# Four fused graph layers on one core: the rounds beside each loop move into it

## The chip, the core and the metric

The kernel runs on one core of a Trainium2 chip. The metric is the device time in microseconds (us) of one execution of the whole program: 2837.21 us, the median of 3 runs (2833.33 to 2839.98). Durations below come from one more execution, the profiled one, which took 2840.6 us, of which 2838.8 us are the span from the first to the last instruction of the program.

The engines are named as in the profile: PE is the matrix engine (PEld its weight loads), DVE, ACT and POOL are the vector, scalar and general engines, SP is the engine that issues the DMAs here.

## What is computed

The input is x of 128 graphs with 64 nodes and 384 features, and a 0/1 adjacency of 64x64 for each graph. Four layers follow one another, each of this form:

```
h = maximum(layernorm(x), 0)
x = x + layer(h, adj)
```

- Layer 0, twice over: `u = h @ (h @ W_left.T).T` above and on the diagonal, the same with `W_right` below it, scaled; `exp(u) * adj` divided by its row sum; times `h @ W_lin.T + b`; layer norm, gain, bias, relu.
- Layers 1 and 2: attention with 12 heads, `q, k, v = h @ Wq.T, h @ Wk.T, h @ Wv.T + bv`, scores `q k / sqrt(384) + bias` with the adjacency as the bias, softmax, times v, then `@ Wo.T + bo`.
- Layer 3, twice over: softmax of `h h / sqrt(384)`, times adj and normalized; three projections of h, one for the part above the diagonal, one for it, one for below; their sum, layer norm, relu.

All is float32. The projections keep float32 accuracy by splitting each operand into a high and a low part and adding three products (`exact_product`, line 229 holds its matmul).

## The kernel before

**Tiles and rounds.** 256 tokens (4 graphs) are a group; there are 32 groups. Two streams (0 and 1) work side by side, each with its own buffers (`wide0`, `ps0` and so on); a round takes one group of each stream, so each layer (a "phase") has ITER = 16 rounds, numbered 0 to 15.

**The order of the work** is written out by hand. For every phase and each of PE, ACT, DVE, POOL there is one line of words (GCN0_ORDERS, ATT_ORDERS, GCN3_ORDERS), each word a stage of one stream; a prime means that the stage belongs to the round before (it is late by one). A BETWEEN line per engine weaves the last late stages of one phase with round 0 of the next. Engines meet only through semaphores, and `Count` works out from the orders which value a wait needs. In the two attention phases the PE's line runs, for each stream, `k2 pv scores` in a row: `pv` (line 1167) and `scores` (line 1136) are 96 small matmuls each in the trace, with 96 weight loads each.

**What is written out and what is looped.** `run_first` emits the not-late stages of round 0. `run_middle` emits round 1, then for phases 0 to 2 `meanwhile` (the split of the next phase's first two weight matrices into high and low part, lines 268 and 276, where PRESPLIT names any: in phases 1 and 2), then round 2, then a hardware loop over rounds 3 to 14, then round 15. Within a loop the round number is in a register, so that each wait against a round's count needs register instructions ahead of it; in a written-out round it is a constant. SP has its own program, `move_program`: it writes out `turn(2)` and loops over 3 to 15. The end of a phase is in `run_between`.

**What each engine runs** is thus, for a phase: round 1, round 2, one loop body passed 12 times, round 15, the between line. PE's copy of a round is by far the longest: 540 matmuls in phase 0, 600 in phases 1 and 2, 404 in phase 3, each with a weight load of its own as an instruction. PE's whole program before the change has 21,828 instructions; ACT, DVE, POOL and SP together have 3,929.

Of the kernel before, what the change touches and what calls it, by code (L numbers as in the profile page):

```python
# [14 lines left out]
ITER = GROUPS // STREAMS  # L15
# [162 lines left out]
def run_middle(eng, order, todo, meanwhile=None):  # L178

    order = [(todo[stage], s, late) for stage, s, late in order]  # L180

    def round_of(r):
        for stage, s, late in order:
            stage(s, r - late)
    round_of(1)
    if meanwhile is not None:
        meanwhile()
    round_of(2)
    with eng.Fori(3, ITER - 1) as r:
        round_of(r)  # L190
    round_of(ITER - 1)


def run_between(line, ended, begun):
# [92 lines left out]
def raw_weights(sp, g, phase):  # L287

    sp.wait_ge(g.hi_split[phase - 1], len(SLOTS[phase - 1]))
    sp.wait_ge(g.lo_split[phase - 1], len(SLOTS[phase - 1]))  # L290
    sp.dma_start(g.w_raw[:], g.weights[phase][:, :STAGED]).then_inc(g.weights_in[phase], 16)


def more_raw_weights(sp, g, phase):

    if len(SLOTS[phase]) > STAGED:
        n = len(SLOTS[phase]) - STAGED
        sp.wait_ge(g.hi_split[phase], n)
        sp.wait_ge(g.lo_split[phase], n)
        sp.dma_start(g.w_raw[:, 0:n], g.weights[phase][:, STAGED:]).then_inc(g.more_weights_in[phase], 16)  # L300


def move_program(sp, g, ph, phases):


    phase, sems, nxt = ph.phase, ph.sems, ph.phase + 1
    before = phases[phase - 1] if phase else None

    def load(s, i, of=phase):
        group = i * STREAMS + s  # L310
        x_in, adj, kinds = g.sources[of]
        if of > phase:
            ph.adj_free(sp, s, ITER - 1)
        elif not isinstance(i, int) or i > 0:
            ph.adj_free(sp, s, i - 1)
        sp.dma_start(g.adjin[s][:, 0:len(kinds)], adj[group][:, kinds[0]:kinds[-1] + 1:kinds.step])\
            .then_inc(g.adj_in[of][s], 16)
        if of > phase:
            ph.x_free(sp, s, ITER - 1)
        elif not isinstance(i, int) or i > 0:  # L320
            ph.x_free(sp, s, i - 1)
        sp.dma_start(g.xin[s][:], x_in[group]).then_inc(g.x_in[of][s], 16)

    def store_and_reload(s, i):
        ph.x_new(sp, s, i)
        sp.dma_start(ph.x_out[i * STREAMS + s], ph.bufs[s].xout).then_inc(sems.stored[s], 16)
        if ph.reload and (not isinstance(i, int) or i + 1 < ITER):
            x_again(s, i + 1)

    def x_again(s, i):  # L330
        sp.dma_start(ph.bufs[s].x, g.sources[phase][0][i * STREAMS + s]).then_inc(sems.x_again[s], 16)

    if phase == 0:
        for s in range(STREAMS):
            load(s, 0)
        for dst, src in ph.params:
            sp.dma_start(dst, src).then_inc(sems.params_in, 16)
    if ph.reload:
        for s in range(STREAMS):
            ph.x_space(sp, s)  # L340
            x_again(s, 0)
    if phase == 0:
        more_raw_weights(sp, g, 0)
    for s in range(STREAMS):
        if before is not None:
            sp.wait_ge(before.sems.stored[s], 16 * ITER + 1)
        load(s, 1)
    if nxt < len(SLOTS):
        for dst, src in phases[nxt].params:
            sp.dma_start(dst, src).then_inc(phases[nxt].sems.params_in, 16)  # L350
        raw_weights(sp, g, nxt)

    def turn(i):
        for s in range(STREAMS):
            store_and_reload(s, i - 2)
            load(s, i)
    turn(2)
    with sp.Fori(3, ITER) as i:
        turn(i)
    if phase and nxt < len(SLOTS):  # L360
        more_raw_weights(sp, g, nxt)
    for s in range(STREAMS):
        store_and_reload(s, ITER - 2)
        if nxt < len(SLOTS):
            sp.wait_ge(sems.stored[s], 16 * (ITER - 2) + 1)
            load(s, 0, of=nxt)
    for s in range(STREAMS):
        store_and_reload(s, ITER - 1)
# [1314 lines left out]
def graph_stack(nc, x, adj, w0, w1, w2, w3, rows0, rows1, rows2, rows3, cols0, cols3, ident, tri, eye, parts,  # L1683
                out):

    with ExitStack() as ctx:
# [56 lines left out]
        def run(eng, k, weights=None):  # L1743

            todo = [dict(ph.stages[k](eng), weights=weights and (lambda m, n=n: weights(n, m)))
                    for n, ph in enumerate(phases)]
            run_first(phases[0].orders[k], todo[0])
            for n, ph in enumerate(phases):
                def meanwhile(to=n + 1):
                    if weights:  # L1750
                        for m in PRESPLIT[to]:
                            weights(to, m)
                run_middle(eng, ph.orders[k], todo[n], meanwhile if n + 1 < len(phases) else None)
                if n + 1 < len(phases):
                    run_between(BETWEEN[n][k], todo[n], todo[n + 1])
            run_last(phases[-1].orders[k], todo[-1])

        @block.sync
        def _(sp):
            sp.dma_start(g.w_raw[:], g.weights[0][:, :STAGED]).then_inc(g.weights_in[0], 16)  # L1760
            for dst, src in g.const_loads:
                sp.dma_start(dst, src).then_inc(g.const_in, 16)
            for ph in phases:
                move_program(sp, g, ph, phases)
            for s in range(STREAMS):
                sp.wait_ge(phases[-1].sems.stored[s], 16 * ITER + 1)
# [94 lines left out]
```

## Time and profile before

| | before |
|---|---|
| median of 3 runs | 2837.21 us |
| lowest, highest | 2833.33, 2839.98 us |
| profiled execution, its span | 2840.6 us, 2838.8 us |
| granted clock of PE, mean over the span | 0.992 of full speed |
| PE busy | 2745.5 us (97%), 34,304 matmuls |
| PEld busy | 2543.5 us (90%) |
| DVE, ACT, POOL busy | 2027.2 (71%), 1283.6 (45%), 1427.2 us (50%) |
| instructions fetched by DMA queue 8 | 85 packets, 1.39 MB |
| instructions fetched by DMA queue 14 | 29 packets, 0.24 MB |

How to read it: busy time is the sum over an engine's own instructions; waits, branches and register instructions are not in it. "issue" as the cause of an idle stretch means that no semaphore ended it: the engine stood still while its sequencer had nothing ready for it. PEclk is the share of full clock that the chip granted PE: 1.0 is 2.4 GHz and 0.5 is 1.2 GHz. Queue 8 and queue 14 carry instructions, not data.

Phase 0 runs from 0 to about 800 us, phase 1 (attention) to about 1400, phase 2 (attention) to about 1985, phase 3 to the end. Windows are cut at the start of PE's loop body, or at the same place of a round that is written out.

### The profile page before, as it was taken

The numbers are of one execution on the slowest core, as the hardware profiler recorded it, in microseconds if no ns is written. First come the engines' busy times: TensorE is split into PE (matmuls) and PEld (weight loads), VectorE is DVE, ScalarE is ACT, GpSimd is POOL, SyncE is SP. The second block draws the span as 40 slices with busy tenths as digits, with TensorE's granted clock in tenths as the row PEclk, the third lists the DMA queues.
The fourth block names the chain that finished last, engine by engine and source line by source line (L and its number), as shares of the span: only waits on it lengthen the run. The fifth ranks groups of instructions, "written<-read, shape, count | busy, mean of one in ns | idle before, by whom it ended". The sixth has DMA issues, their size and how long they took to land.

```text
span 2838.8 us, 85292 instructions
## 1 busy us (share of the span) xinstructions
PE 2745.5 (97%) x34304; PEld 2543.5 (90%) x34304; DVE 2027.2 (71%) x3996; ACT 1283.6 (45%) x2069; POOL 1427.2 (50%) x2507
## 2 busy tenths in 40 slices
PE   6999999999998999999989999999999999999997
PEld 6999999999988999999989999999888888888886
DVE  4666666666686777777767777777677767666776
ACT  3333333333344444444444444444544545445453
POOL 1212112121224555555535555555677777777777
PEclk9999999999999999999999999999999999999999
DMA  4111121211112111111131111112112112111121
GB/s 153 42 62 61 43 79 41 81 41 61 62 54 83 43 48 48 48 49 49 48 100 43 48 48 49 51 51 66 41 39 75 37 37 74 37 64 47 37 74 34
DMA packets 116530, 159.51 MB, mean 56 GB/s; under 512 B 8000, under 2 KB 112320, under 8 KB 116416
## 3 DMA queue, kind: packets, MB, share of 16 engines
q1 hardware_dynamic: 116416, 157.88, 16.9%
q8 instruction: 85, 1.39, 0.2%
q14 instruction: 29, 0.24, 0.0%
HBM read 107.52 MB, written 50.33 MB: 56 GB/s over the span
## 4 chain that ended last, share of the span: by engine, by line
PE 56%; POOL 22%; issue 11%; DVE 5%; ACT 2%; DMA 2%; SPq 1%; POOLq 0%; DVEq 0%; ACTq 0%
PE ps L229 40%; POOL wide L1318 5%; POOL wide L909 4%; POOL wide L900 3%; PE ps L1136 3%; PE ps L1167 2%; PE ps L762 2%; PE ps L1153 2%; PE ps L785 2%; PE ps L702 2%; ACT wide L972 1%; POOL wide L1303 1%; POOL wide L1307 1%; PE ps L1648 1%; POOL x_rstd L867 1%
## 5 line engine op out<-in xcount | busy, mean ns | idle before, releaser
L229 PE MATMUL ps<-w_hi,split 128*128 128x384 f32 x4608 | 1271.8, 344 | 7.6 <-ACT wide L938 4.3
L229 PEld LDWEIGHTS ps<-w_hi,split 128*128 128x128 f32 x4608 | 850.7, 190 | 19.3 <-ACT wide L938 4.7
L229 PE MATMUL ps<-split,w_hi 128*128 128x256 f32 x4608 | 863.8, 283 | 1.6 <-DVE split L619 1.6
L229 PE MATMUL ps<-w_lo,split 128*128 128x384 f32 x2304 | 780.6, 339 | 0.0
L229 PEld LDWEIGHTS ps<-split,w_hi 128*128 128x128 f32 x4608 | 723.8, 189 | 23.9 <-issue 12.7
L229 PE MATMUL ps<-split,w_lo 128*128 128x256 f32 x2304 | 575.6, 280 | 0.0
L229 PEld LDWEIGHTS ps<-w_lo,split 128*128 128x128 f32 x2304 | 438.2, 190 | 1.2 <-issue 1.2
L229 PEld LDWEIGHTS ps<-split,w_lo 128*128 128x128 f32 x2304 | 435.4, 189 | 0.0
L909 POOL TENSOR_TENSOR wide<-wide 128x192 f32<-128x192 f32 x256 | 206.6, 836 | 424.1 <-ACT wide L972 424.1
L1318 POOL TENSOR_TENSOR wide<-wide,row 128x192 f32<-128x192 f32 x512 | 308.9, 637 | 32.5 <-ACT wide L1401 32.5
L496 POOL TENSOR_TENSOR rstd<-mv,pos_half 128x2 f32<-128x2 f32 x64 | 44.2, 699 | 450.6 <-DVE mv L670 450.6
L1401 ACT ACTIVATE wide<-ps 128x768 f32<-128x768 f32 x128 | 103.4, 808 | 250.3 <-PE ps L229 250.3
L900 POOL TENSOR_TENSOR wide<-wide,heads 128x512 f32<-128x512 f32 x128 | 163.2, 1294 | 83.9 <-DVE heads L1040 83.8
L972 ACT ACTIVATE wide<-ps 128x768 f32<-128x768 f32 x64 | 52.0, 812 | 257.2 <-PE ps L229 257.2
L958 ACT ACTIVATE wide<-ps 128x512 f32<-128x512 f32 x192 | 110.1, 598 | 106.7 <-PE ps L1153 62.6
L1053 DVE TENSOR_TENSOR split<-ps,split 128x384 fp32r<-128x384 f32 x128 | 65.4, 553 | 127.5 <-ACT split L967 127.5
L892 POOL TENSOR_TENSOR wide<-xin,bo_row 128x192 f32<-128x192 f32 x256 | 147.4, 605 | 6.3 <-DMA x_after<-wide 6.3
L948 ACT ACTIVATE wide<-wide 128x1536 f32<-128x1536 f32 x64 | 95.3, 1490 | 91.5 <-DVE wide L1023 91.5
L1153 PE MATMUL ps<-ident,wide 128*128 128x128 f32 x768 | 119.2, 282 | 15.0 <-DVE wide L1045 7.2
L1012 DVE TENSOR_TENSOR wide<-ps,bias 128x1536 f32<-128x1536 f32 x64 | 112.0, 1750 | 24.9 <-PE ps L1136 24.9
L923 ACT ACTIVATE wide<-xin,x_shift,x_rstd 128x384 f32<-128x384 f32 x128 | 83.7, 701 | 101.3 <-POOL x_shift L870 101.3
L1464 DVE CAST split<-wide 128x768 fp32r<-128x768 f32 x64 | 42.4, 663 | 113.4 <-ACT wide L1365 68.9
(129 smaller groups left out, 4554.7 us busy)
## 6 DMA issues: line engine op xcount, KB each, us to landing
x_after<-wide SPq DMA_DIRECT2D x96, 384.0 KB, 2.5
xin<-x_after SPq DMA_DIRECT2D x96, 384.0 KB, 3.4
xin<-in_x SPq DMA_DIRECT2D x32, 384.0 KB, 4.3
wide<-in_x SPq DMA_DIRECT2D x32, 384.0 KB, 3.7
wide<-x_after SPq DMA_DIRECT2D x32, 384.0 KB, 4.1
out<-wide SPq DMA_DIRECT2D x32, 384.0 KB, 2.8
w_raw<-in_w SPq DMA_DIRECT2D x4, 2304.0 KB, 12.5
adjin<-in_adj SPq DMA_DIRECT2D x32, 256.0 KB, 3.8
```

The source lines that it names most:

```text
L229: last = nc.tensor.matmul(out, t if tokens_stay else w, w if tokens_stay else t, start=(k == 0), stop=(k == len(pairs) - 1))
L892: ins = nc.gpsimd.tensor_tensor(b.xout[:, rows, at], b.xin[:, rows, at], bo_row[:, at], ALU.add)
L900: nc.gpsimd.tensor_tensor(b.e_rows[:, c * n:(c + 1) * n], b.e_rows[:, c * n:(c + 1) * n], b.factor[:, c * n:(c + 1) * n].unsqueeze(2).broa ...
L909: ins = nc.gpsimd.tensor_tensor(b.xout[:, rows, at], b.xout[:, rows, at], b.o_raw[:, rows, at], ALU.add)
L923: ins = nc.scalar.activation(b.h[:, t], b.xin[:, t], ACT.Relu, bias=b.x_shift[:, t:t + 1], scale=b.x_rstd[:, t:t + 1])
L948: nc.scalar.activation(b.e[:], b.e[:], ACT.Exp, scale=SCALE).then_inc(act_done[s], 1)
L958: nc.scalar.activation(b.pT[:, HPC * c:HPC * c + HPC], b.ps[:, c % 2, :], ACT.Copy)\
L1012: nc.vector.tensor_tensor(b.s[:].rearrange("p c r k -> p r c k"), b.ps[:, :, 0:C * P].rearrange("p r (c k) -> p r c k", c=C), b.bias[:].re ...
L1136: mm = nc.tensor.matmul(b.ps[t * NODES:(t + 1) * NODES, r, c * P + gr * NODES:c * P + (gr + 1) * NODES], b.q[r * HD:(r + 1) * HD, c, at:at ...
L1153: mm = nc.tensor.transpose(b.ps[:, c % 2, r * P:(r + 1) * P], b.e[:, c, r], g.ident[:])
L1318: ins = nc.gpsimd.tensor_tensor(b.hw[:, rows, m, at], b.hw[:, rows, m, at], w_row[l][m][:, at], ALU.add)
L1401: nc.scalar.activation(b.hw[:, :, m], b.ps_w[m], ACT.Copy).then_inc(act_done[s], 1)
```

## The change

The written-out copies of round 2 and round 15 are removed, on all engines and in all four phases, and the loop runs over 2 to 15 in their place; on SP `turn(2)` goes into its loop. Round 0, round 1, `meanwhile` and the between lines stay written out. No stage, tile or dependency changes, and no wait gets another value. The program gets shorter: PE's from 21,828 to 13,172 instructions, those of the other four from 3,929 to 2,649.

```
@@ -185,10 +185,8 @@
     round_of(1)
     if meanwhile is not None:
         meanwhile()
-    round_of(2)
-    with eng.Fori(3, ITER - 1) as r:
+    with eng.Fori(2, ITER) as r:
         round_of(r)
-    round_of(ITER - 1)
 
 
 def run_between(line, ended, begun):
@@ -354,8 +352,7 @@
         for s in range(STREAMS):
             store_and_reload(s, i - 2)
             load(s, i)
-    turn(2)
-    with sp.Fori(3, ITER) as i:
+    with sp.Fori(2, ITER) as i:
         turn(i)
     if phase and nxt < len(SLOTS):
         more_raw_weights(sp, g, nxt)
```

Two places show what stands where. Line numbers of the changed kernel are 2 to 3 lower. The first is ACT in phase 1, around the end of round 1; L268 (L266) is the high part of the next phase's weights, L948 (L945) the exponential, L938 (L935) the copy of q, L923 (L920) the norm. Before, written-out round 2 follows the weights:

```order
L972 ACTIVATE wide1<-ps1 128x768
L948 ACTIVATE wide0<-wide0 128x1536
L268 ACTIVATE w_hi<-w_raw 128x1152 x2
L938 ACTIVATE wide1<-ps1 128x768
L923 ACTIVATE wide0<-xin0,x_shift0,x_rstd0 128x384 x2
L958 ACTIVATE wide0<-ps0 128x512
```

Now the loop begins right behind them, and its first pass is round 2:

```order
L969 ACTIVATE wide1<-ps1 128x768
L945 ACTIVATE wide0<-wide0 128x1536
L266 ACTIVATE w_hi<-w_raw 128x1152 x2
L188 UNCONDITIONAL_BRANCH
L188 ISA
L935 ACTIVATE wide1<-ps1 128x768
L914 REGISTER_ALU
L916 ISA
L920 ACTIVATE wide0<-xin0,x_shift0,x_rstd0 128x384 x2
```

The weights keep their place between round 1 and round 2; the rows that are new behind them are the loop's register instructions. The second place is PE in phase 2, behind the loop's end, from the last product of v on (48 in these rows are 96 matmuls in the trace). Before, this is written-out round 15, with its `pt`, `hT`, `k2`, then `pv` and `scores`:

```order
L229 MATMUL ps1<-w_hi,split1_1 128x384 x3
L1153 MATMUL ps0<-ident,wide0 128x128 x4
L1072 MATMUL ps0<-ident,wide0 128x128 x6
L1153 MATMUL ps0<-ident,wide0 128x128 x8
L229 MATMUL ps1<-split1_0,w_hi 128x256
L229 MATMUL ps1<-split1_0,w_lo 128x256
L229 MATMUL ps1<-split1_0,w_hi 128x256
L229 MATMUL ps1<-split1_0,w_lo 128x256
L229 MATMUL ps1<-split1_0,w_hi 128x256
L229 MATMUL ps1<-split1_0,w_lo 128x256
L229 MATMUL ps1<-split1_1,w_hi 128x256 x3
L1167 MATMUL ps0<-wide0 32x64 x48
```

Now it is the between line to phase 3, which stood one round further down before:

```order
L227 MATMUL ps1<-w_hi,split1_1 128x384 x3
L227 MATMUL ps1<-split1_0,w_hi 128x256
L227 MATMUL ps1<-split1_0,w_lo 128x256
L227 MATMUL ps1<-split1_0,w_hi 128x256
L227 MATMUL ps1<-split1_0,w_lo 128x256
L227 MATMUL ps1<-split1_0,w_hi 128x256
L227 MATMUL ps1<-split1_0,w_lo 128x256
L227 MATMUL ps1<-split1_1,w_hi 128x256 x3
L1133 MATMUL ps1<-wide1 64x64 x48
L1150 MATMUL ps0<-ident,wide0 128x128 x12
L1164 MATMUL ps0<-wide0 32x64 x48
```

One written-out stretch with `pv` and `scores` of both streams is gone from behind the loop, and one from ahead of it.

## Rows read from the trace of the kernel before

**Rows 1.** The page: PE's busy time, and the queue with PE's instructions.
```profile
PE 2745.5 (97%) x34304; PEld 2543.5 (90%) x34304; DVE 2027.2 (71%) x3996; ACT 1283.6 (45%) x2069; POOL 1427.2 (50%) x2507
q8 instruction: 85, 1.39, 0.2%
```

**Rows 2.** Phase 1, rounds 1-4, 15: window, length, PE/PEld/DVE/ACT/POOL busy (count), PEclk, DMA, GB/s.
```profile
837.40:878.10 40.70, 34.81 (x614) 33.45 (x606) 28.50 (x35) 15.94 (x23) 15.95 (x26) 0.94 0.38 123
878.10:926.70 48.60, 39.91 (x601) 38.60 (x601) 30.42 (x37) 18.91 (x26) 17.42 (x30) 0.89 0.12 37
926.70:963.60 36.90, 35.28 (x601) 34.22 (x601) 27.11 (x35) 16.82 (x24) 18.60 (x30) 0.98 0.15 47
963.60:998.50 34.90, 34.68 (x603) 33.59 (x602) 27.46 (x35) 16.77 (x24) 19.61 (x30) 1.00 0.14 40
1348.10:1383.20 35.10, 34.77 (x602) 33.66 (x601) 27.62 (x35) 16.79 (x24) 19.53 (x30) 1.00 0.16 53
```

**Rows 3.** Phase 2, rounds 1, 2, 3, 4, 15, the same columns.
```profile
1424.10:1465.20 41.10, 34.98 (x617) 33.17 (x610) 28.12 (x35) 16.03 (x24) 18.48 (x30) 0.94 0.44 141
1465.20:1507.80 42.60, 37.48 (x601) 36.08 (x600) 29.90 (x37) 18.97 (x26) 18.67 (x30) 0.93 0.15 45
1507.80:1546.30 38.50, 36.31 (x602) 35.25 (x602) 27.80 (x35) 16.71 (x24) 18.60 (x30) 0.95 0.16 53
1546.30:1582.20 35.90, 35.81 (x601) 34.89 (x601) 27.11 (x34) 16.72 (x24) 18.55 (x30) 0.96 0.11 37
1931.80:1968.50 36.70, 34.78 (x602) 33.64 (x601) 27.62 (x35) 16.78 (x24) 19.54 (x30) 1.00 0.25 84
```

**Rows 4.** Phase 1, rounds 1 and 2 (837.4 to 926.7): instruction packets of queue 8.
```profile
q8 instruction: 10, 0.16, 0.8%
```

**Rows 5.** Phase 1, rounds 4 to 14 (963.6 to 1348.1): the same.
```profile
q8 instruction: 1, 0.02, 0.0%
```

**Rows 6.** PEld in time, round 14 of phase 1: start, length, line, count.
```profile
1345.34 1.01 PEld L1167 LDWEIGHTS ps<-wide 64*32 64x32 f32 x96
1346.44 1.12 PEld L1136 LDWEIGHTS ps<-wide 32*64 32x64 f32 x96
```

**Rows 7.** The chain of work, 880 to 930 us: start, length, what.
```profile
884.17 1.16 ACT w_hi L268
885.35 2.81 DVE w_lo L276 x2
...
901.08 2.26 issue
...
921.96 2.90 issue
```

**Rows 8.** PEld's waits, phase 1, 837.4 to 1383.2: total, times, longest.
```profile
PEld ps L1136 <- issue: 11.3, 6, 3.0
```

**Rows 9.** PEld's waits, phase 2, 1424.1 to 1968.5.
```profile
PEld ps L1136 <- issue: 9.6, 5, 2.2
PEld ps L1153 <- DVE wide L1045: 6.0, 12, 3.7
```

**Rows 10.** Phase 0, round 2 (written out) and round 4 (in the loop).
```profile
86.70:136.40 49.70, 49.70 (x542) 45.62 (x541) 33.18 (x89) 19.36 (x37) 10.57 (x24) 1.00 0.18 60
186.00:235.70 49.70, 49.70 (x541) 45.63 (x541) 33.29 (x89) 19.35 (x37) 10.59 (x24) 1.00 0.18 58
```

**Rows 11.** Phase 3, rounds 2, 3 and 14.
```profile
2093.90:2145.70 51.80, 51.03 (x405) 45.10 (x404) 36.61 (x92) 25.86 (x44) 39.23 (x71) 1.00 0.16 52
2145.70:2197.30 51.60, 51.11 (x406) 45.16 (x405) 36.54 (x93) 25.85 (x44) 39.47 (x72) 1.00 0.16 52
2712.00:2763.50 51.50, 51.02 (x407) 45.25 (x406) 36.50 (x92) 25.84 (x45) 39.61 (x75) 1.00 0.15 51
```

**Rows 12.** The loop's own instructions on PE: count, shortest/median/longest in ns.
```profile
L189 PEldq ALU_OP  x48: 32/32/32, 185.7 to 2763.2; - x48
L189 PEldq COMPARE_BRANCH  x48: 76/208/247, 185.8 to 2763.3; - x48
```

More of the change, by code:

```diff
@@ L187, in run_middle @@
         meanwhile()
-    round_of(2)
-    with eng.Fori(3, ITER - 1) as r:
+    with eng.Fori(2, ITER) as r:
         round_of(r)
-    round_of(ITER - 1)
 def run_between(line, ended, begun):
@@ L356, in turn @@
             load(s, i)
-    turn(2)
-    with sp.Fori(3, ITER) as i:
+    with sp.Fori(2, ITER) as i:
         turn(i)
```

## The prediction

> **What bounds the kernel now.** I read the page first. PE is busy 97% of the span [rows 1], at full clock nearly everywhere, so nothing on DVE, ACT or POOL matters unless PE waits for it; the question is where PE's missing 3% lies and whether this change reaches it. The page also lists a queue that fetches instructions: 85 packets for 1.39 MB, 16 KB each [rows 1]. PE's program has 21,828 instructions, so one packet holds about 256 of them, and 85 packets are the program once. PE executes over 68,000 matmuls and weight loads, three times the program. So a loop's later passes are not fetched again.
>
> Next the windows by round. In phase 1 the ordinary round takes 34.9 us (round 4) [rows 2], but round 2 takes 48.6 and round 3 takes 36.9, with the same count of 600 matmuls. In phase 2 rounds 2, 3, 4 and 15 take 42.6, 38.5, 35.9 and 36.7 [rows 3]. The same work is slow at the start of each attention phase and becomes even a few rounds on. The DMA view says what differs: 10 instruction packets arrive in rounds 1 and 2 [rows 4], one in the eleven rounds 4 to 14 [rows 5]. Round 3 is the loop's first pass and is fetched like written-out code.
>
> Then the chain of waits. In round 2 it holds two stretches of "issue", 2.26 and 2.90 us [rows 7], where no semaphore is awaited. Both stand inside `scores`. The waits view adds them up: PEld before L1136 stood on "issue" for 11.3 us in 6 stops in phase 1 [rows 8] and 9.6 us in 5 stops in phase 2 [rows 9]. Why there: `pv` and `scores` together issue 192 weight loads and 192 matmuls in 2.2 us [rows 6]. A packet's worth of instructions is eaten in 1.5 us there, where a whole round of some 1,215 instructions takes 34.9. After such a stop PE's clock falls from 2.4 to 1.2 GHz for a stretch; round 2 of phase 1 has a mean of 0.89 [rows 2], which is 0.11 x 48.6 = 5.3 us of full-speed work lost in that round.
>
> One more thing lies in round 2, and is not the fetch: the split of the next phase's weights, 1.16 us on ACT and 2.81 us on DVE [rows 7], sits ahead of round 2's softmax on their queues; PE's transposes (L1153) wait 3.7 us for it in phase 2 [rows 9].
>
> At the fetch the Trainium skill (Runtime: NRT & Kernel Launch, "Instruction fetch mechanics") says that blocks are 16 KiB, 256 instructions, which agrees with 1.39 MB in 85 packets. It also says that crossing a block's border is mostly hidden; by that this change would be worth nothing. The trace decides against it for code as dense as `pv` and `scores`: stops of 2.26 and 2.90 us.
>
> **Part 1: rounds 2 and 15 are no longer fetched as code of their own.** Time over 34.9 us:
> - phase 1: round 2 13.7, round 3 2.0, round 4 0, round 15 0.2, sum 15.9 [rows 2];
> - phase 2: 7.7, 3.6, 1.0, 1.8, sum 14.1 [rows 3].
>
> Together 30.0 us. The weight split stays (it stands between round 1 and the loop on ACT and DVE in the new order too). It costs about 4.8 us a phase: 3.7 to 4.0 us of wait and some 1 us of half clock behind it; the second number is my choice, from the way round 2 falls behind an ordinary round. That leaves 30.0 - 9.6 = 20.4 us for the fetch, in six fetched rounds (2, 3 and 15 of two phases): 3.4 us each, between 0.2 (round 15 of phase 1) and 8.9 (round 2 of phase 1).
>
> Now round 2 is the loop's first pass, fetched once, and rounds 3 to 15 come from what is held. Fetched rounds go from six to two. At the mean, 2 x 3.4 = 6.8 us remain: 13.6 us less. Bounds: with 0.2 each, 20.0 less; with 8.9 each, 2.6 less.
>
> I checked the mean by position, since a stop can only come where PE reaches the border between two packets. I counted PE's instructions from the start of the program to each load that ended such a stop (the ones after 2.26 and 2.90 us, and eight more in the two phases): all leave the same remainder, 232 or 233, on division by 256. Taking the removed copies out (1,088 instructions each in phase 0, 1,215 in phases 1 and 2) moves the borders. By the new count round 1 of phase 1 keeps one stop of its two, its round 2 gets two small ones (0.9 and 1.6 us), phase 2 keeps both in round 1 and has one of 2.0 and one of 0.4 us in round 2. Stops in all, at the length that the trace's stops have: 11.6 us, where the same count gives 19.6 for the kernel before. With fewer stretches of half clock this comes out at 12 to 15 us. I stay with the mean.
>
> **Part 2: the other phases.** In phase 0 a written-out round takes 49.7 us and one in the loop 49.7 [rows 10]: nothing is lost to the fetch, since its densest stages are short; worth 0. In phase 3 rounds 2 and 3 take 51.8 and 51.6, a later one 51.5 [rows 11]: 0.2 us less at most.
>
> **Part 3: what the loop adds.** Eight more rounds (two in each of four phases) carry register instructions on every engine. On PE the branch takes 208 ns and a register instruction 32 ns [rows 12]; by the program's count a round in the loop has 16 to 26 instructions more, so at most 8 x (0.21 + 26 x 0.032) = 8.3 us if all of it were exposed. Cover: PE's sequencer runs ahead of the matmuls, and the two equal rounds of phase 0 [rows 10], with 26 such instructions in one and none in the other, show 0. I take 0. DVE, ACT and POOL are busy 27, 17 and 20 us of 34.9 [rows 2], so their register instructions fall into idle time. SP gains one looped turn per phase; its loads are for a round ahead and nothing waits for them there.
>
> **Sum.** -13.6 - 0.2 + 0 = -13.8, rounded to -14. Against the profiled execution, 2840.6 us: 2826.6. The runs' median is 3.4 us below the profiled one, so 2837.2 - 14 = 2823 us.
>
> **Rivals.**
> - *The remaining fetched rounds are the bad ones.* A phase's first rounds are where the raw weights arrive (123 and 141 GB/s in round 1 [rows 2, 3], 37 to 53 later) and packets may be late behind them; round 2 of phase 1 was the worst of all. If the two first passes cost 8.9 and 6 us, or if PE, no longer held up, waits for DVE and ACT instead, the change brings 20.4 - 14.9 = 5 us: 2832. Against it: round 2's own bytes are few (37 GB/s), DVE and ACT have 7 and 18 us to spare.
> - *They are nearly free*, as round 15 of phase 1 was: -20 us, 2817. It needs luck with the borders in both phases.
> - *The register instructions are exposed* in the attention phases, where the queue ahead of PE is emptied in `scores`: 4 rounds x 1 us and some more where a wait's value comes late, up to 8 us of the 14 given back: 2831. Against it: round 4 is a loop round and takes 34.9 us, written-out round 15 of phase 1 35.1 [rows 2].
> - *Slower: a loop no longer stays held.* What is held must cover the loop body (1,232 instructions in attention, 4.8 packets, so up to 6) and what is read beyond its end. If the shifted borders break this for one loop, each of its 13 later passes is fetched: 13 x 3.4 = 44 us, less the 14: 2867. It decides at the point where one pass has to drop the loop's first packet. Against it: both attention loops touch six packets' worth of code before and after, and phase 0's five now instead of six. The Trainium skill's same section speaks for this rival: it says only two blocks are held and that a taken branch out of them forces a fetch before execution goes on. By it the eight added passes would each stop at least once, by the stops seen 8 x 2.3 = 18 us. But 11 passes of a loop of 4.8 packets brought one packet [rows 5], so the trace does not bear that out.
>
> **Chances.** Forecast 0.70, bad ones 0.12, nearly free 0.10, exposed registers 0.05, loop not held 0.03. About 0.2%, 5.7 us, is what a measurement of this kernel can tell from no change. The forecast's own range is 2818 to 2829; the nearly free case lies at 2817 and the bad ones at 2832, so 2816 to 2831 holds 8 in 10. Faster by over 0.2%: nearly all of the forecast, the free case, a third of the others, 0.83. Within: 0.13. Slower: the last rival and a little, 0.04.
>
> **What the changed profile would show.** Queue 8 has 51 or 52 packets (13,172 / 256) and 0.84 MB. Windows: round 2 of the attention phases is still long (38 to 45 us with the weight split), round 3 and round 15 take 34.9 to 35.1. PEld's "issue" before L1133 (1136 before) falls from 11 stops to 5 to 7 in the phases' loops and round 1. Phase 0 and phase 3 keep their length within 0.5 us. The mean granted clock rises from 0.992 to 0.994 or more. I am wrong if round 3 or 15 is still long, if packets arrive during the loops' later passes, or if the time saved there comes back as PE's waits for DVE or ACT.

## The result, and the profile after

The changed kernel took 2827.53 us, the median of 6 runs (2824.36 to 2828.89), beside 2837.59 us for the kernel before on the same chip (6 runs, 2833.33 to 2841.05). The ratio is 0.9956, with a 95% interval of 0.9944 to 0.9968: 9 to 16 us less. Run again in the second group of experiments, it stood at 0.9963 (0.9950 to 0.9976). The forecast of 14 us less is a ratio of 0.9951, inside the first interval and at the edge of the second. The profiled execution took 2825.8 us, 14.8 us less than the profiled one of before; the medians differ by 10 and 9 us. So the direction and the place were right, and the size was some 2 to 4 us too large. The ratios and intervals below leave out three executions, one each of round 15 alone, round 2 alone and all but PE, which took 9203 to 9204 us at full clock, for a reason that no trace here shows.

The page of the changed kernel, the same lines as [rows 1]:

```profile
span 2824.0 us, 86094 instructions
PE 2738.9 (97%) x34304; PEld 2534.4 (90%) x34304; DVE 2026.3 (72%) x3996; ACT 1282.2 (45%) x2069; POOL 1432.6 (51%) x2507
q8 instruction: 51, 0.84, 0.1%
```

PE's fetch has fallen from 85 packets to 51, the number that the prediction worked out from the length of the program. PE is busy for 6.6 us less, though it does the same work. That is about what fewer stretches at half clock would give: from 830 to 2000 us ten such stretches hold 33.6 us of busy PE before and six hold 20.2 us now, and half of the difference is 6.7 us. The mean granted clock rose from 0.992 to 0.995.

The windows of phase 1, rounds 1, 2, 3, 4 and 15, which answer to [rows 2] (length; PE, PEld, DVE, ACT, POOL busy with counts; PEclk; DMA share; GB/s):

```profile
836.10:874.00 37.90, 34.43 (x619) 33.08 (x612) 28.14 (x35) 15.94 (x23) 16.30 (x26) 0.95 0.42 131
874.00:916.40 42.40, 35.61 (x602) 33.55 (x600) 31.23 (x37) 18.97 (x26) 19.83 (x30) 1.00 0.14 43
916.40:950.90 34.50, 34.40 (x601) 33.48 (x601) 26.16 (x35) 16.82 (x24) 18.62 (x30) 1.00 0.13 41
950.90:985.90 35.00, 34.71 (x603) 33.49 (x602) 27.57 (x35) 16.82 (x24) 19.72 (x30) 1.00 0.15 48
1335.50:1370.40 34.90, 34.61 (x601) 33.38 (x600) 27.47 (x35) 16.81 (x24) 19.80 (x30) 1.00 0.15 52
```

The same of phase 2, which answers to [rows 3]:

```profile
1409.70:1451.40 41.70, 35.81 (x616) 34.07 (x609) 27.93 (x35) 16.01 (x24) 17.47 (x30) 0.92 0.46 145
1451.40:1496.60 45.20, 38.44 (x602) 37.12 (x601) 30.40 (x37) 19.06 (x26) 17.42 (x30) 0.92 0.13 42
1496.60:1532.50 35.90, 35.80 (x602) 34.88 (x602) 27.18 (x34) 16.71 (x24) 18.61 (x30) 0.96 0.12 38
1532.50:1567.50 35.00, 34.70 (x601) 33.37 (x600) 27.45 (x35) 16.82 (x24) 19.77 (x30) 1.00 0.15 48
1918.20:1953.30 35.10, 34.80 (x602) 33.47 (x602) 27.55 (x35) 16.82 (x24) 19.78 (x30) 1.00 0.26 86
```

Read the two phases apart. In phase 1 round 2 fell from 48.6 to 42.4 us and its clock rose from 0.89 to 1.00, and round 3 fell from 36.9 to 34.5. In phase 2 round 2 *rose* from 42.6 to 45.2, while rounds 3, 4 and 15 fell by 2.6, 0.9 and 1.6. From the start of round 1 to the end of round 15, phase 1 gave 11.5 us (545.8 to 534.3) and phase 2 only 0.8 (544.4 to 543.6). The start up to round 2 of phase 0 gave 1.3, the rest of phase 0 gave 1.1 and phase 3 lost 0.3. One stop of the kernel before escapes these windows: PEld stood on issue for 1.24 us just behind the cut at 1383.2 (next load at 1384.78), so phase 1 with it gave 12.7.

The changed kernel has a second profile (its run beside the experiments), and what differs between the two is not the change. From round 1 to round 15 of phase 1, then of phase 2, then rounds 2 to 15 of phase 0 and 1 to 15 of phase 3:

```profile
838.90:1373.90 535.00, 522.09 (x9019) 502.97 (x9012) 416.09 (x513) 253.63 (x361) 290.70 (x446) 0.99 0.17 54
1413.30:1954.20 540.90, 522.72 (x9014) 502.43 (x9006) 415.79 (x512) 253.56 (x362) 292.61 (x450) 0.99 0.18 57
86.90:782.50 695.60, 695.60 (x7562) 638.59 (x7561) 466.59 (x1233) 271.24 (x505) 148.31 (x336) 1.00 0.18 58
2028.70:2801.00 772.30, 765.35 (x6062) 677.49 (x6061) 544.61 (x1377) 385.69 (x660) 590.53 (x1079) 1.00 0.15 50
```

Here phase 2 gave 3.5 us, phase 0 nothing (695.6 against 695.0 before), and round 2 was 42.7 us at clock 0.92 in phase 1 and 44.2 in phase 2, round 3 34.6 and 34.9. The long round 2 of phase 2 stands in both profiles; a difference of 1 to 3 us in one phase of one profile does not tell kernels apart.

The waits of PEld in phase 1 and then in phase 2, in total, times, longest (L1133 is now `scores`, L1150 the transposes, L227 the large matmuls), which answer to [rows 8] and [rows 9]:

```profile
PEld ps L1133 <- issue: 2.2, 2, 1.4
PEld ps L227 <- issue: 1.3, 1, 1.3
...
PEld ps L1150 <- DVE wide L1042: 8.1, 14, 4.3
PEld ps L1133 <- issue: 5.3, 3, 1.9
PEld ps L227 <- issue: 1.2, 1, 1.2
```

The stops on "issue" before `scores` fell from eleven, 20.9 us in all [rows 8, 9], to five of 7.5 us; with the two before L227 there are seven, 10.0 us. Four of the seven are in phase 2, and they are long. The trace also shows the packet at each of the seven: PE goes on 1.2 to 1.5 us after a packet of queue 8 has ended. Around the stop that ended at 1495.44, for example, one packet started at 1492.87 and took 1.07 us, and no other of that queue from 1488 to 1495.4. Counted over PE's instructions in the trace, the ends of successive stops within a phase lie multiples of 256 apart, to within two.

Not all of the stops' time came off. PE's own waits on issue before `scores` and the large matmuls fell by 10.3 us in the two phases (19.5 to 9.2), its idle time there by 7.8 us (38.0 to 30.2): some 2.5 us came back as other waits.

### The profile page after: what moved, and what is told of

Its sections match the earlier page's. It is cut to its first block, busy times and chain, and to the rows that moved or that the text cites. A ratio compares the mean times of both kernels' runs of the same rounds, so it can differ in the third digit from the quotient of the medians.

```text
span 2824.0 us, 86094 instructions
## 1 busy us (share of the span) xinstructions
PE 2738.9 (97%) x34304; PEld 2534.4 (90%) x34304; DVE 2026.3 (72%) x3996; ACT 1282.2 (45%) x2069; POOL 1432.6 (51%) x2507
## 4 chain that ended last, share of the span: by engine, by line
PE 51%; POOL 26%; issue 13%; DVE 5%; ACT 3%; DMA 2%; POOLq 1%; SPq 0%; DVEq 0%; ACTq 0%
PE ps L227 37%; POOL wide L1315 6%; POOL wide L906 5%; POOL wide L897 4%; PE ps L1133 3%; PE ps L1164 2%; PE ps L759 2%; POOL wide L1300 2%; PE ps L782 2%; POOL wide L1304 2%; PE ps L1150 2%; ACT wide L969 2%; PE ps L699 2%; POOL x_rstd L864 1%; POOL rstd L1334 1%
## 5 line engine op out<-in xcount | busy, mean ns | idle before, releaser
L227 PE MATMUL ps<-w_hi,split 128*128 128x384 f32 x4608 | 1268.2, 343 | 8.7 <-ACT wide L935 5.5
L227 PEld LDWEIGHTS ps<-w_hi,split 128*128 128x128 f32 x4608 | 846.3, 190 | 23.8 <-ACT wide L935 6.1
L227 PE MATMUL ps<-split,w_hi 128*128 128x256 f32 x4608 | 863.5, 283 | 1.6 <-DVE split L616 1.6
L227 PE MATMUL ps<-w_lo,split 128*128 128x384 f32 x2304 | 777.3, 337 | 1.2 <-issue 1.2
L227 PEld LDWEIGHTS ps<-split,w_hi 128*128 128x128 f32 x4608 | 723.5, 189 | 23.9 <-issue 12.7
L227 PE MATMUL ps<-split,w_lo 128*128 128x256 f32 x2304 | 575.2, 280 | 0.0
L227 PEld LDWEIGHTS ps<-w_lo,split 128*128 128x128 f32 x2304 | 436.0, 189 | 0.0
L227 PEld LDWEIGHTS ps<-split,w_lo 128*128 128x128 f32 x2304 | 435.2, 189 | 0.0
L493 POOL TENSOR_TENSOR rstd<-mv,pos_half 128x2 f32<-128x2 f32 x64 | 44.2, 699 | 448.2 <-DVE mv L667 448.2
L945 ACT ACTIVATE wide<-wide 128x1536 f32<-128x1536 f32 x64 | 95.3, 1489 | 96.2 <-DVE wide L1020 96.2
L1150 PE MATMUL ps<-ident,wide 128*128 128x128 f32 x768 | 119.6, 281 | 16.6 <-DVE wide L1042 7.7
L920 ACT ACTIVATE wide<-xin,x_shift,x_rstd 128x384 f32<-128x384 f32 x128 | 83.7, 701 | 102.0 <-POOL x_shift L867 102.0
L1150 PEld LDWEIGHTS ps<-ident,wide 128*128 128x128 f32 x768 | 87.1, 141 | 37.4 <-DVE wide L1042 13.8
## 6 DMA issues: line engine op xcount, KB each, us to landing
w_raw<-in_w SPq DMA_DIRECT2D x4, 2304.0 KB, 11.5
```

Source lines behind the costliest of these rows:

```text
L227: last = nc.tensor.matmul(out, t if tokens_stay else w, w if tokens_stay else t, start=(k == 0), stop=(k == len(pairs) - 1))
L920: ins = nc.scalar.activation(b.h[:, t], b.xin[:, t], ACT.Relu, bias=b.x_shift[:, t:t + 1], scale=b.x_rstd[:, t:t + 1])
L945: nc.scalar.activation(b.e[:], b.e[:], ACT.Exp, scale=SCALE).then_inc(act_done[s], 1)
L1150: mm = nc.tensor.transpose(b.ps[:, c % 2, r * P:(r + 1) * P], b.e[:, c, r], g.ident[:])
```

## The experiments

The twelve runs (eleven edits, and the changed kernel again) stood beside the kernel before, in groups of four on one chip each. On the three chips the kernel before took 2837.93, 2839.06 and 2843.16 us (medians), so I compare ratios. "Stops" below is what the profile gives as PEld's waits on issue before `scores` and before the large matmuls, from 830 to 2000 us. "Half clock" counts the stretches at granted clock 0.5 in the same time (one of double length counts as two).

| kernel | ratio to before (95%) | span | stops, us | half clock |
|---|---|---|---|---|
| before | 1 | 2838.8 | 22.6 | 10 |
| changed | 0.9956 (0.9944-0.9968) | 2824.0 | 10.5 | 6 |
| changed, again | 0.9963 (0.9950-0.9976) | 2824.6 | 10.5 | 4 |
| round 15 alone | 0.9990 (0.9976-1.0003) | 2832.0 | 17.2 | 9 |
| round 2 alone | 0.9991 (0.9979-1.0003) | 2830.1 | 16.4 | 8 |
| PE alone | 0.9951 (0.9936-0.9967) | 2822.4 | 11.0 | 6 |
| all but PE | 1.0025 (1.0012-1.0038) | 2847.4 | 23.9 | 11 |
| changed, 195 ahead | 0.9949 (0.9936-0.9962) | 2820.0 | 5.4 | 4 |
| changed, 51 ahead | 0.9986 (0.9974-0.9999) | 2836.7 | 14.1 | 9 |
| more written out | 1.0109 (1.0089-1.0129) | 2864.3 | 40.5 | 12 |
| small weight split | 0.9934 (0.9915-0.9952) | 2827.1 | 13.5 | 7 |
| before, 195 ahead | 1.0009 (0.9997-1.0021) | 2841.1 | 20.0 | 11 |
| PE alone, 195 ahead | 0.9924 (0.9906-0.9941) | 2818.1 | 6.5 | 4 |
| changed but DVE | 0.9949 (0.9931-0.9967) | 2825.6 | 12.6 | 6 |

The theory, F: PE stands still where it reaches a packet of instructions that has not arrived; only code run for the first time is fetched, and only in `pv` and `scores` does PE eat a packet faster than the next arrives. The rivals are named in the expectations.

**Which engine.** The change was made on PE alone (k is 0 for PE, 1 for ACT, 2 for DVE, 3 for POOL), and then on all engines but PE, with `looped=k != 0` and SP's loop as in the changed kernel:

```
+    if looped:
+        with eng.Fori(2, ITER) as r:
+            round_of(r)
+        return
     round_of(2)
     with eng.Fori(3, ITER - 1) as r:
...
-                run_middle(eng, ph.orders[k], todo[n], meanwhile if n + 1 < len(phases) else None)
+                run_middle(eng, ph.orders[k], todo[n], meanwhile if n + 1 < len(phases) else None,
+                           looped=k == 0)
```

> The change on PE alone: its rounds 2 and 15 go into its loop; ACT, DVE, POOL and SP keep theirs written out. Theory F: all of the change is PE's fetch, so the time is that of the changed kernel, 9 to 12 us less than before, with 51 packets on queue 8 and 29 on queue 14. Theory R (the other engines' part): 0 to 3 us less.

> The change on all engines but PE, whose program stays as before. Theory F: within 2 us of before, 85 packets on queue 8. Theory R (the other engines' part): most of the 10 us less. If the register instructions of the loop cost something on ACT, DVE or POOL, this one is slower than before by it.

PE alone has the whole gain: 0.9951, 13.9 us less by the ratio, which is above the 9 to 12 expected, though its interval and the changed kernel's nearly coincide. All engines but PE is slower than the kernel before, 7 us by the ratio, where F had at most 2: a miss. So the gain is PE's, as F says, and with PE's rounds written out the looped form on the others is not free. But the two do not add up: -13.9 and +7 would make 7 us less, and the changed kernel has 10.5 to 12.5 less. What the others cost beside a looped PE is then less than 7 us, and why it is more beside a written-out one stays open. The part that its trace shows plainly is DVE's, and it is taken up below.

**Which round.** From the kernel before, only round 15 moved into the loop, or only round 2 (with SP's turn 2):

```
-    with eng.Fori(3, ITER - 1) as r:          -    round_of(2)
-        round_of(r)                           -    with eng.Fori(3, ITER - 1) as r:
-    round_of(ITER - 1)                        -        round_of(r)
+    with eng.Fori(3, ITER) as r:              +    with eng.Fori(2, ITER - 1) as r:
+        round_of(r)                           +        round_of(r)
                                                    round_of(ITER - 1)
```

> Only round 15 goes into the loop (3 to 15), round 2 stays written out, on all four engines with orders. Theory F (PE's fetch of code it has not run yet): PE fetches 4 attention rounds per two phases more than the changed kernel does, 2 fewer than before. Taken at the mean, 2 x 3.4 = 6.8 us less than before; taken by what round 15 cost in the trace of before (0.2 + 1.8), 2 us less; by the borders' new positions 16.4 us of stops instead of 18.4, so about 3 less. I expect 2 to 4 us less, queue 8 with 68 packets. Theory R (the loop form itself, the register waits or the other engines' shorter code, is what is faster): half of the changed kernel's 10 us, 5 less.

> Only round 2 goes into the loop (2 to 14), round 15 stays written out; SP as in the changed kernel. Theory F: round 3 comes from what is held. By the rows of before (rounds 3 and 4: 2.0 + 3.6 + 1.0) 6.6 us less than before; by the borders' new positions 15.8 us of stops instead of 18.4, with the clock 4 less. I expect 4 to 7 less and 68 packets, and rounds 3 to 14 at 34.9 to 35.1 us. Theory R: 5 less, and it adds up exactly with the kernel that moves round 15 alone.

By the ratios 2.8 and 2.6 us, neither clear of zero, and together 5.4 where both at once gave 12.5. Both profiles have the 68 packets. The first lies in the 2 to 4 us expected, the second misses its 4 to 7; R's 5 us lies inside both intervals, so these two runs alone do not rule R out (the runs by engine and by position do), but its sum does not hold. A rate of 3.4 us for each fetched round does not describe this: either edit takes two fetched rounds away, which would be 6.8. The stops do describe it. Each edit also moves the borders in all the code behind it, and the stops came down only to 17.2 and 16.4 us, from 22.6; the spans followed, 6.8 and 8.7 us less. The profiled executions show more of the gain than the medians here; each is a single execution, and I can't tell why.

**Where the borders lie.** This needs no round moved. To the changed kernel I added tiny matmuls ahead of PE's program, 49 of them for 195 instructions, 13 for 51:

```
             pe.wait_ge(g.const_in, g.const_count)
+            for _ in range(49):
+                nc.tensor.matmul(g.ps[0][0:HD, 0, 0:1], g.ident[0:HD, 0:HD],
+                                 g.ident[0:HD, 0:1], start=True, stop=True,
+                                 tile_position=(0, 0))
             run(pe, 0)
```

> The changed kernel with 49 tiny matmuls ahead of everything on TensorE, which add 195 instructions there and so move every border of 256 instructions back by 195. Fetch by position (F): a stop comes where a border lies within some 3.4 us of running behind the last one, and that is inside pv and scores. With the borders moved, my count over the round's instructions gives stops of 1.1 and 1.9 us in phase 1 (rounds 1 and 2) and 1.8 and 2.0 us in phase 2, 6.8 us in all against 10.4 us for the changed kernel: 3 to 6 us less than the changed kernel, with fewer stretches at half clock than its six. Rival (cost per fetched instruction, F'): what counts is how many instructions are fetched, 195 more here, wherever the borders lie: 0 to 2 us more than the changed kernel.

> As the run with 195 more instructions, but 13 tiny matmuls, which add 51. F: stops of 1.6, 1.9 and 1.9 us in phase 1, 1.9, 1.9 and 2.1 us in phase 2 and 0.6 us between, 11.9 us in all against 10.4: 0 to 4 us more than the changed kernel. F': within 0.5 us of the changed kernel.

The changed kernel of the same group stood at 0.9963. With 195 ahead it was 0.9949, about 4 us less by ratio and by median (2825.91 against 2830.05); the two intervals overlap, though of the single executions only two of five with 195 ahead are above the fastest of six without. With 51 ahead it was 0.9986, 6.5 us more, and there the intervals lie almost apart, and ten of its eleven executions are above the slowest of the six. The run with 195 answers to its expectation; the run with 51 went the way expected and went further, since one stop was longer than any counted: 3.31 us, in round 1 of phase 1. Its trace, PEld in time (start, length, line, and in brackets the idle time ahead):

```profile
860.83 0.19 PEld L227 LDWEIGHTS ps<-w_hi,split 128*128 128x128 f32 x1 [3.31 <-issue]
```

It follows directly on a whole `pv` and `scores`, in the stretch in which a raw weight matrix of 2304 KB arrives. The kernel with the small weight split, below, has a stop of 2.28 us at 862 us as well, 4 us behind the end of `scores`, and there the DMA engines were 0.98 busy:

```profile
861.00:864.60 3.60, 1.41 (x11) 1.32 (x11) 3.56 (x4) 1.37 (x2) 2.01 (x2) 1.00 0.98 314
```

The columns are those of the windows above. What PE ran right ahead of the stop were large matmuls, 11 with 1.4 us of busy time, not the dense ones. So a packet may also be late because the queues are full of weights, which the prediction had as the ground for its rival of 5 us; two stops that coincide with a load do not show it. In the changed kernel's two profiles no such stop is there, though the same load passes.

The filler itself is not the cause. In front of the kernel before it does nothing that can be told:

> The kernel before with the same 49 tiny matmuls (195 instructions) ahead of TensorE's program that took 4 us off the changed kernel. F: with ten rounds' worth of fetched attention code the borders fall into pv and scores somewhere wherever they start; my count gives 18.4 us of stops at either position, so within 3 us of the kernel before. Rival (the filler itself helps, by warming something at the start, or by reordering the start): 3 to 5 us less than the kernel before, as there.

1.0009, within the 3 us that F left it: with twice the fetched attention code the borders hit `pv` and `scores` somewhere from either start (20.0 us of stops against 22.6). Its span is 2.3 us longer all the same: differences of that size between single executions are not explained by the stops.

**More of the same.** From the kernel before, rounds 3, 4, 13 and 14 written out too:

```
-    round_of(2)
-    with eng.Fori(3, ITER - 1) as r:
+    for r in (2, 3, 4):
+        round_of(r)
+    with eng.Fori(5, ITER - 3) as r:
         round_of(r)
-    round_of(ITER - 1)
+    for r in (ITER - 3, ITER - 2, ITER - 1):
+        round_of(r)
```

> The change turned round: from the kernel before, rounds 3, 4, 13 and 14 are written out too, on all engines, so that four more rounds of each phase are fetched. F: stops of 36 us against 18 us in the kernel before, and half-clock stretches behind them: 18 to 28 us more than the kernel before, about 2860 us; by the forecast's own 3.4 us for each fetched round of phases 1 and 2 it is 8 x 3.4 = 27 us more. TensorE's packets rise from 85 to about 119, and each added round of phases 1 and 2 is at least 1.5 us over the looped ones. Rival G (what the looped rounds save is not the fetch but a one-time effect at the border of loop and written-out code): there are as many such borders as before, so within 4 us of the kernel before.

1.0109 (1.0089 to 1.0129): 25 to 37 us more, 31 at the middle, and 25.5 in the spans. Rival G is out. F's 18 to 28 us was a little low, as the stops were (40.5 us where 36 were counted); 31 us over eight rounds is 3.9 each, 25.5 is 3.2, on either side of the 3.4 in the prediction. My expectation of 119 packets was a slip: it left out the rounds of phases 0 and 3. The page has 152, and 85 + 4 x (1,088 + 2 x 1,215 + about 815) / 256 is that. One more part of the expectation missed: not every added round is 1.5 us over a looped one, since round 14 of phase 2 took 34.7 us and round 13 of phase 1 41.1. It depends on where a border falls. Its queue line, its waits, and two of the added rounds (3 and 14 of phase 1, windows as above):

```profile
q8 instruction: 152, 2.49, 0.4%
```

```profile
PEld ps L1138 <- issue: 36.8, 22, 3.2
```

```profile
923.20:961.80 38.60, 36.72 (x601) 35.67 (x600) 27.17 (x35) 16.77 (x24) 18.48 (x30) 0.94 0.14 46
1325.50:1362.60 37.10, 35.43 (x601) 34.37 (x601) 27.22 (x35) 16.87 (x24) 18.60 (x30) 0.98 0.15 48
```

Round 14, looped at 35.0 us in the kernel before, takes 37.1 written out. It is the cleanest single reading of the mechanism: same work, far from any weight load or phase start, 2.1 us more, and a mean clock below 1.

**The weight split.** In the changed kernel, DVE and ACT split only 16 of the 384 columns of the first two weights of phases 2 and 3; the rest of these two matrices stays unsplit, so this part of the computation is left out.

```
+    cut = slice(0, 16) if phase >= 2 and m in PRESPLIT[phase] else slice(0, FEAT)
+    nc.scalar.activation(g.w_hi[:, at, :, cut], g.w_raw[:, m % STAGED, :, cut], ACT.Copy).then_inc(g.hi_split[phase], 1)
...
-    nc.vector.tensor_tensor(g.w_lo[:, at], g.w_raw[:, m % STAGED], g.w_hi[:, at].bitcast(F32),
+    nc.vector.tensor_tensor(g.w_lo[:, at, :, cut], g.w_raw[:, m % STAGED, :, cut],
+                            g.w_hi[:, at, :, cut].bitcast(F32),
```

> The changed kernel in which VectorE and ScalarE split only 16 of the 384 columns of the first two weights of phases 2 and 3 (the ones split between rounds 1 and 2 of the phase ahead); the rest of these two weights is left unsplit, so the kernel leaves that part of the computation out. The forecast's term for this split was 4.8 us in each of phases 1 and 2, read as the wait of pt (TensorE for VectorE) in round 2, which was 3.7 and 4.2 us in the changed kernel. If that term is of the right size and only the weight split stands there: 7 to 10 us less than the changed kernel, and the pt wait of round 2 gone. Rival (the borders' stops in round 2 take the time when the wait goes, since TensorE then runs through pv and scores sooner after the last border): 2 to 6 us less.

0.9934 (0.9915 to 0.9952) against 0.9956 and 0.9963 for the changed kernel: 6 to 8 us between the middles, with overlapping intervals and on another chip, across the border of my two cases (2 to 6 and 7 to 10) and not decided. The wait before the transposes in round 2 fell from 3.7 to 1.1 us in phase 1 and from 4.3 to 1.9 in phase 2. Round 2 of the two phases, against 42.4 and 45.2:

```profile
882.30:923.30 41.00, 36.93 (x602) 35.06 (x602) 29.75 (x38) 17.13 (x26) 18.83 (x30) 0.96 0.14 44
1460.60:1499.70 39.10, 35.85 (x601) 34.28 (x600) 28.06 (x37) 17.20 (x26) 18.52 (x30) 0.98 0.13 42
```

1.4 and 6.1 us less. But its span, 2827.1, is 3 us *over* that of the changed kernel, because round 1 of phase 1 was 5 us longer in this execution, with the stop behind the weight load shown above. One profile can't tell a term of this size; that a split costs some 3 to 4 us a phase fits the waits and the ratios, and is not shown closer than that.

**DVE's loop.** In phase 2 a looped round takes 35.07 us in the changed kernel and 34.95 in the kernel before. Rounds 4 to 15 of the changed kernel, and the same rounds with the change on PE alone, windows as above:

```profile
1532.50:1953.30 420.80, 417.24 (x7202) 401.21 (x7201) 330.27 (x409) 201.77 (x288) 237.31 (x360) 1.00 0.16 52
```

```profile
1533.70:1953.10 419.40, 415.86 (x7202) 401.16 (x7201) 330.29 (x409) 201.90 (x288) 237.83 (x360) 1.00 0.16 52
```

Between two rounds laid side by side the first difference is on DVE: what follows the reciprocal starts later. In the kernel before, then in the changed one (start, length, line):

```profile
1732.02 0.30 DVE L1037 RECIPROCAL heads<-heads 128x24 f32<-128x24 f32 x1
1732.45 0.19 DVE L1040 SCALAR_TENSOR_TENSOR heads<-heads 128x24 f32<-128x24 f32 x1
```

```profile
1752.83 0.30 DVE L1034 RECIPROCAL heads<-heads 128x24 f32<-128x24 f32 x1
1753.37 0.18 DVE L1037 SCALAR_TENSOR_TENSOR heads<-heads 128x24 f32<-128x24 f32 x1 [0.23 <-DVE heads L1034]
```

0.13 us between the end of the one and the start of the other, then 0.23; PE's transposes wait for exactly this chain. So the changed kernel was run with DVE's rounds 2 and the last written out as before (`looped=k != 2`):

> The changed kernel with VectorE's rounds 2 and the last written out as in the kernel before. In phase 2 of the changed kernel each looped round took 35.07 us, in the kernel before 34.95, and so it did where only TensorE was changed: VectorE's scalar_tensor_tensor behind its reciprocal starts 0.11 us later in every such round. If it is VectorE's loop in its new place: 34.95 us again, 14 x 0.12 = 1.7 us less than the changed kernel. If the cause is another engine's loop: 35.07 us stay, and the time is within 1 us of the changed kernel.

Rounds 4 to 15 of phase 2, the same window:

```profile
1536.70:1956.10 419.40, 415.95 (x7202) 401.31 (x7201) 330.33 (x409) 202.15 (x288) 237.34 (x360) 1.00 0.16 52
```

419.4 us: the 1.4 us are DVE's. The time, 0.9949 (0.9931 to 0.9967), lies on the side expected, though a difference of 1.7 us is below what these runs can tell. It isn't the loop as such: with only round 15 or only round 2 moved, DVE loops too, and the round stays at 34.96 us; and in phase 1 of the changed kernel, the same code on DVE, rounds 5 to 14 take 349.6 us as in the kernel before. All profiles agree: the six kernels or repeats with DVE's program as in the changed kernel have 35.06 to 35.07 us and 0.23 us behind the reciprocal in phase 2, the seven others that can be compared 34.95 to 34.97 and 0.12. What differs is where DVE's code of this loop lies in its program. I didn't test that.

**The fastest version.** The experiments point to one: the change on PE alone, with the 195 instructions ahead.

> The change on TensorE alone (all other engines and the sync queue as in the kernel before), with the 195 instructions ahead. If the two are additive (the change on TensorE alone was 13.8 us under the kernel before, the changed kernel 10 us, and the 195 instructions took 4 us off the changed kernel): 15 to 18 us less than the kernel before, about 2821 us, the fastest so far. If the change on TensorE alone was only ahead by chance of the borders' positions: 12 to 14 us less.

0.9924 (0.9906 to 0.9941), 2821.04 against 2843.16 us: 17 to 27 us less than the kernel before. That is the fastest kernel of the study and goes beyond the additive case (15 to 18 us expected, 21.6 at the middle). Its interval lies below that of the changed kernel; with that of the change on PE alone it overlaps slightly. The filler is bound to this program's length: any edit ahead of the attention loops moves the borders again.

## Why the prediction was right, and where its numbers were off

**Part 1, the mechanism: shown.** PE alone carries the gain; each stop ends just behind a packet, a multiple of 256 instructions after the last; writing out more rounds costs 3.2 to 3.9 us each; moving the borders alone moves the time by 4 us down and 6 us up. Over the profiles of the table, thirteen without the kernel that leaves work out, span against stops lies on a line of 1.36 us for each us of stop (it accounts for 94% of the variance). The 0.36 beyond the stop itself is about what the half-clock stretches behind the stops cost; that part is argued from the table, not tried by itself. By that slope the change in stops, 22.6 to 10.5, is worth 16.5 us; 14.8 came between the spans, 10 between the medians.

**Part 1, the positions: shown.** The prediction had one stop in round 1 of phase 1, two small ones of 0.9 and 1.6 us in round 2, two in round 1 of phase 2, and 2.0 and 0.4 us in its round 2. The trace has 1.43; 0.82 and 1.31; 1.70 and 1.73; 1.85 and 1.20. All seven are at remainder 232 or 233 on division by 256. The sum is 10.0 us where 11.6 was counted. The second profile has six of the seven at the same places, 1.2 to 2.1 us long. One of the long ones, PEld in time, the last of round 2 in phase 2:

```profile
1495.44 0.58 PEld L1133 LDWEIGHTS ps<-wide 32*64 32x64 f32 x40 [1.85 <-issue]
```

**Part 1, the mean of 3.4 us: right in the sum, wrong as a rate.** Of the 20.4 us in rounds 2, 3 and 15, 13.6 were to go. By the same excess over 34.9 us 8.8 went in phase 1 (15.9 to 7.1) and 2.5 in phase 2 (14.1 to 11.6), 11.3 in all, and round 1 of the two phases gave another 2.2, which the term did not have. The lower bound of 0.2 us a round came from round 15 of phase 1, whose stop of 1.24 us lay just behind the window's cut; the rival of the free rounds rested on the same number. That phase 2 gained so little (0.8 us from round 1 to 15, 3.5 in the second profile) is what the rival of the bad rounds said, for one phase of the two. What the first profile shows for it is the borders: round 2 of phase 2 had one stop and now has two, and its wait for the weight split came out 0.6 us longer (4.3 against 3.7). The runs of round 15 alone and round 2 alone show the same: a rate per round is a mean over positions, and one edit is one draw from it. They gave 1.3 to 1.4 us for each fetched round. That the mean met the change's own size this well is in part luck.

**Part 1, the weight split, 4.8 us a phase: fair.** It stayed, as said: 3.7 and 4.3 us of wait in the changed kernel. Its removal was worth 6 to 8 us by the ratios in both phases together, where 9.6 were set down; so it may be over by a few us, and the fetch under by as much.

**Part 2: right.** Phase 3 is at 772.6 against 772.3 us. Phase 0 is 1.1 us shorter over rounds 2 to 15 (693.9 against 695.0), where 0 was forecast with 0.5 of play, but 0.6 longer in the second profile (695.6): the 1.1 us belong to the execution, not to the change.

**Part 3, the loop's own instructions at 0: wrong for DVE, the one step that was.** PE's were free, as the two equal rounds of phase 0 said. For the others I argued from busy time (DVE 27 of 34.9 us), and that was the wrong measure: DVE's chain from reciprocal to transpose is waited for by PE in every round, so 0.11 us there goes through whatever the idle time elsewhere. In phase 2 that is 14 x 0.12 = 1.7 us. The change on PE alone has 540.2 us in phase 2, where the changed kernel has 543.6 and, in its second profile, 540.9; more than the 1.7 us is not shown by them. That the engines other than PE took 7 us when they changed alone points the same way, but of that 7 only 1.7 can be read at a place. The stops are 1.3 us longer (23.9 against 22.6), and phase 3 took 774.4 against 772.3 us; but it took 774.6 too in the kernel before with the filler, whose other engines are unchanged. The rest stays open.

**The rivals.** Nearly free and loop not held are out: round 2 is still long, and in phase 1 rounds 4 to 14 still bring one packet. Registers exposed was right in kind, on DVE, not on PE, and small. The Trainium skill (Runtime: NRT & Kernel Launch, "Instruction fetch mechanics") warns that a taken branch out of two held blocks forces a fetch. By that the looped rounds would stop, and the trace shows none. The same section also gives PE a larger instruction memory than the other engines, 2048 instructions, and the trace agrees with that: 1,232 stay held. Its sentence that a border is mostly hidden holds in phase 0 and not in `scores`.

**The signs set down beforehand.** The packets (51), the five stops before L1133 and the mean clock (0.995) came as said. Round 2 of phase 2 was just above its 38 to 45 us (45.2; 44.2 in the second profile). Round 3 left its 34.9 to 35.1: 34.5 in phase 1, and 35.9 in phase 2 at a mean clock of 0.96, but 34.9 in the second profile. The time that came back as PE's other waits, the last sign of being wrong, was there in part: 2.5 us of 10.3.

## What to carry to other kernels

Where a loop's first rounds are slow and its later ones even, look for waits on "issue" inside the densest small-tile code, and for the instruction queue's packets: written-out copies of a dense loop body cost their fetch each time, here 1.3 to 3.9 us per copy in the mean of an edit, and by the slope above about a quarter of that behind the stops, where PE ran at half clock. Count borders (256 instructions) through the program before you move code: an edit that takes copies out also moves every border behind it, and that alone was worth 4 us down or 6 us up, half the edit. For an engine that isn't the bound, ask whether the bound engine waits on the chain that you touch, not how busy the engine is.

## What the runs showed of the chip that I had not expected

- Filler of 195 instructions ahead of a program took 4 us off it, and 51 added 6, by position alone. The stops in these kernels were 0.8 to 3.3 us long.
- Two long stops coincided with a weight load: 3.31 us directly behind `scores`, and 2.28 us in large matmuls, with the DMA engines 0.98 busy. The changed kernel's two executions passed the second place without one. That the load made the packet late is likely, not shown. This may be a part of the spread between runs of one kernel (2824 to 2834 us for the changed one), which no run here settles.
- The same DVE instructions in the same loop, at another place in DVE's program, took 0.11 us longer at one point of every pass, in all six profiles of that program.
